# Moving the bias addition of five quads of the first block from ScalarE to VectorE, in a fused cross-attention and FP4 feed-forward kernel

## The reference, cut to what matters

```python
# x: (2, 2048, 512), ctx_1024: (2, 77, 512)
def xattn(features, textual_features, q_masks, Ws, W, w, b, Wcw, bcw, Wcb, bcb):
    txt_proj = einsum('btd,de->bte', textual_features, Ws)
    feat_proj = einsum('bfd,de->bfe', features, W)
    h = tanh(txt_proj[:, None, :, :] + feat_proj[:, :, None, :] + b)      # (2, 2048, 77, 512)
    rho = einsum('bftd,d->bft', h, w[:, 0]) + (1 - q_masks) * NEG
    att = softmax(rho, axis=-1)
    txt_h = einsum('bft,btd->bfd', att, textual_features)
    return tanh(txt_h @ Wcw.T + bcw) * features + tanh(txt_h @ Wcb.T + bcb)

def ffn(x, w_gate, w_up, w_down):            # w_gate, w_up: (1408, 512), w_down: (512, 1408)
    q = fp4_quant_dequant                    # blocks of 16 along the last dim
    h = silu(q(x) @ q(w_gate).T) * (q(x) @ q(w_up).T)
    return q(h) @ q(w_down).T

x = x + xattn(layernorm(x), ctx_1024, ...)
return x + ffn(layernorm(x), w_gate, w_up, w_down)
```

## Time and profile before

| | |
|---|---|
| median of 3 runs | 1590.9 us (1589.16 to 1591.69) |
| the profiled execution | 1591.61 us |
| its span, first to last instruction | 1589.8 us |
| busy: PE / ACT / DVE / POOL | 1452.7 / 1365.2 / 1196.1 / 243.0 us |
| mean granted TensorE clock | 0.976 of 2.4 GHz |
| chain that ended last, by engine | PE 56%, ACT 32%, DVE 9% |

### The profile page before, as it was taken

One profiled execution on the slowest core, in us unless ns is written; L12 is line 12 of the kernel. 1 busy time (PEld: TensorE's weight loads), 2 busy tenths in 40 slices (PEclk: granted clock), 3 DMA queues, 4 the chain that ended last, 5 costly groups with the idle time before them and its releaser, 6 DMA issues.

```text
span 1589.8 us, 24376 instructions
## 1 busy us (share of the span) xinstructions
PE 1452.7 (91%) x9752; PEld 643.9 (41%) x9752; DVE 1196.1 (75%) x1964; ACT 1365.2 (86%) x1258; POOL 243.0 (15%) x406
## 2 busy tenths in 40 slices
PE   6978888866999899997999999899999999889998
PEld 3334444411333333343434444344444444445554
DVE  6599998765586566768676776788878777788887
ACT  5999999999999899998999999989999999233331
POOL 1132222110111011111011111101101111012111
PEclk9989999988999999999999999999999999999999
DMA  4133333230011111202111111111111121123322
GB/s 141 40 80 81 86 80 79 70 75 18 8 26 39 35 30 39 39 14 39 39 39 38 40 39 39 29 36 39 39 39 39 39 39 39 39 52 77 77 66 61
DMA packets 180790, 77.91 MB, mean 49 GB/s; under 512 B 163883, under 2 KB 163883, under 8 KB 180677
## 3 DMA queue, kind: packets, MB, share of 16 engines
q1 hardware_dynamic: 179984, 75.00, 21.0%
q10 hardware_dynamic: 693, 1.36, 0.2%
HBM read 27.85 MB, written 8.39 MB: 23 GB/s over the span
## 4 chain that ended last, share of the span: by engine, by line
PE 56%; ACT 32%; DVE 9%; issue 1%; DMA 1%; POOL 0%; SPq 0%; ACTq 0%; DVEq 0%; POOLq 0%
PE rho L745 20%; ACT hring L570 20%; PE dn L834 9%; ACT hring L565 6%; PE gu0g L822 5%; PE gu1g L822 4%; PE gu0u L822 4%; PE gu1u L822 4%; ACT featT L570 4%; PE gu1u L772 1%; PE gu1g L772 1%; PE gu0u L772 1%; PE gu0g L772 1%; DVE featT L909 1%; ACT featT L565 1%
## 5 line engine op out<-in xcount | busy, mean ns | idle before, releaser
L570 ACT ACTIVATE hring<-featT,bias 128x1024 f32<-128x1024 f32 x880 | 929.6, 1154 | 21.7 <-PE rho L745 21.7
L745 PE MATMUL rho<-hring,wslide 128*32 128x512 f32 x4112 | 507.7, 618 | 86.0 <-ACT hring L570 76.9
L745 PEld LDWEIGHTS rho<-hring,wslide 128*32 128x32 f32 x4112 | 113.4, 111 | 382.5 <-issue 208.6
L834 PE MATMUL dn<-wd_room,turned 128*128 128x512 f16 x1023 | 233.3, 380 | 0.0
L470 POOL TENSOR_SCALAR split_t<-sm 128x88 f32<-128x88 f32 (+2 forms) x91 | 22.4, 246 | 1194.1 <-DVE sm L931 1194.0
L909 DVE TENSOR_SCALAR featT<-featT,bias 128x1024 f32<-128x1024 f32 x264 | 181.0, 749 | 8.2 <-ACT featT L570 3.6
L1210 DVE TENSOR_TENSOR work<-sg,gu1u 128x352 f32<-128x352 f32 x64 | 33.4, 521 | 175.6 <-ACT sg L603 175.2
L834 PEld LDWEIGHTS dn<-wd_room,turned 128*128 128x128 f16 x1023 | 95.2, 98 | 155.5 <-issue 51.1
L822 PE MATMUL gu0g<-wg,turned 128*128 128x352 f16 x768 | 127.6, 317 | 9.6 <-DVE work L1210 8.5
L565 ACT ACTIVATE hring<-featT 128x4096 f32<-128x4096 f32 x35 | 126.6, 3617 | 7.6 <-DVE featT L909 7.6
L822 PE MATMUL gu1g<-wg,turned 128*128 128x352 f16 x768 | 127.0, 316 | 4.8 <-DVE work L1210 4.8
(11 more groups left out here) (192 smaller groups left out, 1523.7 us busy)
## 6 DMA issues: line engine op xcount, KB each, us to landing
xt<-in_x SPq DMA_DIRECT2D x32, 256.0 KB, 2.8
out<-xt SPq DMA_DIRECT2D x32, 256.0 KB, 2.4
work<-in_x SPq DMA_DIRECT2D x10, 512.0 KB, 3.7
xt<-in_x SPq DMA_DIRECT2D x6, 512.0 KB, 3.9
xt<-in_L_ffn_w_gate SPq DMA_DIRECT2D x11, 256.0 KB, 2.6
xt<-in_L_ffn_w_up SPq DMA_DIRECT2D x11, 256.0 KB, 2.7
work<-in_L_ffn_w_down SPq DMA_DIRECT2D x2, 704.0 KB, 4.4
xt<-in_L_ffn_w_down SPq DMA_DIRECT2D x2, 704.0 KB, 4.2
```

The lines of the kernel that those rows point to most:

```text
L570: act.activation(slot[s][:, g, :], featT[:, e, ROW0[k]:ROW0[k] + rows], ACT.Tanh, bias=bias[:, e, base + tok:base + tok + 1]).then_inc(tan ...
L745: last = pe.matmul(rho[SLOTW * g:SLOTW * g + SLOTW, hf * 512:hf * 512 + 512], wslide[:, e, SLOTW - 1 - r:2 * SLOTW - 1 - r], slot[s][:, g, ...
L834: last = pe.matmul(dn[:, :], hqT[:, a, c, :], wd[:, bb, c, :], start=(c == 0 and i == 0), stop=(c == NC - 1 and i == 2))
```

## The change

Five quads of block 0, the numbers 18, 27, 36, 45 and 54 (`HEAD_SUMS`), become summed quads. VectorE makes each sum in a new function `head_sum()`, four TENSOR_SCALARs of 128 x 1024 into `wd_room` (`head_room`), in the rounds w = 1, 3, 5, 7 and 9 between gate_up_weights(w+1, 0) and stats_pair(w+1). ScalarE takes such a quad with one ACTIVATE of 128 x 4096 from there, after it has waited for `summed`. The one room serves all five, so each sum waits until the tanh of the one before is through; and SP's first turning of the down weights into `wd_room` waits for the tanh of quad 54. Blocks 1 to 3 keep the summed quads and the rooms that they had.

```diff
     summed_quads, room_of, room_from = [], {}, {}
+    HEAD_SUMS = [14 + 9 * w // 2 for w in range(1, 10, 2)]
+    for i, m in enumerate(HEAD_SUMS):
+        summed_quads.append(m)
+        room_of[m], room_from[m] = -1, HEAD_SUMS[i - 1] if i > 0 else None
     last_in = {r: QPB * (r + 1) - 1 for r in range(NBLK)}
+    OTHERS = len(HEAD_SUMS)
...
-            room = 0 if k == 1 else 1 + len(summed_quads) % (k - 1)
+            room = 0 if k == 1 else 1 + (len(summed_quads) - OTHERS) % (k - 1)
...
+        head_room = wd_room[:, 0:4096].rearrange("p (g c) -> p g c", g=GRP)
...
             load_wd(1)
+            sp.wait_ge(tanh_ready, GRP * (HEAD_SUMS[-1] + 1))
             for r in range(KC):
                 sp.wait_ge(wdq_ready, r + 1)
...
                 if n in SUMMED:
                     act.wait_ge(summed, GRP * (SUMMED[n] + 1))
                     r = ROW0[room_of[n]]
-                    act.activation(slot[s], featT[:, :, r:r + rows], ACT.Tanh).then_inc(tanh_ready, GRP)
+                    added = featT[:, :, r:r + rows] if room_of[n] >= 0 else head_room
+                    act.activation(slot[s], added, ACT.Tanh).then_inc(tanh_ready, GRP)
                     return
...
+            def head_sum():
+
+                n = summed_quads[sums[0]]
+                if room_from[n] is None:
+                    dve.wait_ge(first_ready, 1)
+                else:
+                    dve.wait_ge(tanh_ready, GRP * (room_from[n] + 1))
+                for g in range(GRP):
+                    r, e = quad_at(n)
+                    dve.tensor_scalar(head_room[:, g, :], featT[:, e, 0:BLOCKS[0]],
+                                      bias[:, e, GRP * r + g:GRP * r + g + 1], None, ALU.add).then_inc(summed, 1)
+                sums[0] += 1
...
             for w in range(NC - 1):
                 copy_pair(w)
                 gate_up_weights(w + 1, 0)
+                if w % 2 == 1:
+                    head_sum()
                 stats_pair(w + 1)
```

## The result

The changed kernel takes 1598.64 us (median of 5 runs, 1597.34 to 1600.07) against 1589.16 for the kernel before in the same series. The medians are 9.5 us apart; the ratio on record is 1.0052, 95% interval 1.0041 to 1.0064, which makes 8.3 us (6.5 to 10.2). The forecast was 6.9 us and 1598; the absolute time is hit more closely than the difference, since the kernel before had 1590.9 us in the series on which the forecast rests. The profiled execution has a span of 1596.8 us, 7.0 longer.

The account below looks back on a forecast made before the run. In the first block VectorE's loop, as long as ScalarE's and TensorE's, would set the pace. Debt of 11.65 us less 3.38 slack less 1.35 regained gives 6.9 us; 1590.9 + 6.9 = 1597.8, said as 1598, range 1594.8 to 1602.5.

Parts of the forecast that it names:

- VectorE's loop as the bound: First block's rounds: VectorE's 19.34 us equal ScalarE's and TensorE's to 0.15 us, so with the sums VectorE sets the pace.
- The debt at turning 10: Five sums of 2.75 us less 2.1 us of waits make stats_pair(10) 11.65 us late; less 3.38 slack, turning 10 8.27.
- ScalarE's gain of 0: Five summed quads save ScalarE at most 3.35 us, which turn into waiting for TensorE, so 0 is taken.
- The 1.35 us regained behind turning 10: From turning 10 to quad 58: 13.95 us instead of 15.3, so quad 58 is late by 6.9 us, not 8.27.
- the rival of the lower clock: Scores behind TensorE's waits run at 1.2 GHz; behind turning 10 this adds 0.6 to 1.6 us; 1600 to 1601, 12%.
- TensorE with 2 us to spare at the even turnings: Five quads need about 20.0 us against VectorE's 22.1, so TensorE waits there 2.1 us for GpSimd.
- turning 10 alone with its 3.4 us of slack decides: At the last turning with a sum, 11.65 us of debt less 3.38 of slack sets the delay carried on.
- The waits that pay for part of the debt: VectorE's former waits for TensorE, 1.0, 0.5 and 0.6 us ahead of rounds 2, 6, 8, take 2.1 us off the debt.
- The rest moves along: Behind quad 58, the softmax and the rest of the kernel move by the same 6.9 us.
- features_pair(9): Behind turning 10: its 5.26 us wait for TensorE absorbs the rest of VectorE's debt, leaving some 0.5 us of wait.
- VectorE's slack covers the sums: Rival: each sum only uses its even turning's 3.38 us and VectorE catches up; ScalarE's saving remains, 1587.6 us, 5%.
- ScalarE waits for the sum: Rival at quad 54: costs nothing until a sum is 3.6 us longer; then a microsecond more, 2%.

Follow-up runs that it names:

- pool_root: Changed kernel with its five sums, but GpSimd makes the three Newton steps of each pair's reciprocal root ahead of its normalising; ratio 1.0075 to the kernel before.
- sums_only: Changed kernel, but ScalarE ignores VectorE's five sums in block 0 and keeps four biased ACTIVATEs a quad; 1599.34 against 1590.19 us before, ratio 1.0056.
- three_sums: Changed kernel with only the first three sums (quads 18, 27, 36; rounds 1, 3, 5); ratio 1.0040 to the kernel before, 6.4 us.
- one_sum: Changed kernel with only the first sum (quad 18, round 1); ratio 1.0017 to the kernel before, 2.7 us.
- act_only: Changed kernel without VectorE's sums in block 0; ScalarE takes the five quads in one ACTIVATE each, biases left out; 1589.42 against 1590.19 us before, ratio 0.9995.

## Why the prediction was right, and where its steps were off

**VectorE's loop as the bound: right in the main.** That a 91% busy engine had no room was read from its waits and its round of 19.34 us. VectorE's half alone costs as much as the whole change, and with another 1.2 us taken from each round the same five sums cost nothing. pool_root shows the limit: there VectorE's round has less work, and the kernel is slower.

**The debt at turning 10: right in size.** Forecast 11.65 us at the end of stats_pair(10), measured 274.06 - 262.82 = 11.2; a sum is 2.65, not 2.75. Turning 10 was to be 8.27 us late and is 8.35 (276.31 - 267.96).

**ScalarE's gain of 0: right within the measurement.** sums_only and the changed kernel differ by less than their intervals; alone it is 0.8 us, at most 2.2. The forecast had ScalarE's waits for TensorE grow by about 10 us in the first block; from 94 to 366 us they grew by 10.8, from 10.2 to 21.0.

**The 1.35 us regained behind turning 10: wrong in size.** It was to be 13.95 us from the turning to quad 58; it took 291.27 - 276.31 = 15.0, mainly since the turning ran at the lower clock (1.9 us instead of 1.1); the rest are a score of 1.92 and 0.15 us up to ScalarE's start, which the sum left out. So 0.35 came back and quad 58 is 8.0 late instead of 6.9. That is the rival of the lower clock, forecast at 0.6 to 1.6 us.

**TensorE with 2 us to spare at the even turnings: wrong.** I had reckoned 20.0 us for five quads at full clock; from turning 5 to turning 6 it took 22.0 (193.16 - 171.16): 1.4 of the 2.0 us more are the score behind the wait, which took 3.31, and 0.3 the projection behind it. So the even turnings didn't wait for GpSimd, only once for 0.5 us, and the waits sum to 12.4 us from turning 2 on, not 15 to 20. The end didn't suffer, since VectorE's round of 22.0 was as long. But the step behind it, that turning 10 alone with its 3.4 us of slack decides, is what three_sums refutes (6.4 us against the 1.5 of that formula). What three_sums showed in its place: each late odd turning pushes TensorE and ScalarE back, and they don't make it up by turning 10. In the changed kernel turning 9 is 7.8 us late already, and turning 10 finds its pair ready 0.5 us before. With five sums both ways of reckoning give nearly the same number, and that this one came out is luck.

**The waits that pay for part of the debt: not sound.** 2.1 us came from an execution with turning 1 at the lower clock; another has 0.2. Against that one, quad 58 of the changed kernel is 10.4 us late (291.27 - 280.91), not 8.0. So the forecast of 6.9 us is low by this term, and the measured 8.3 us is between the two. That one_sum costs 2.7 us fits this, but was not shown apart.

**The rest moves along: right up to the softmax (8.0 us), and nearly to the end.** The profiled pair ends 7.0 apart, the timed runs 8.3 by their ratio. What took 1.7 us back between the two stores shown stays open.

**features_pair(9): too little left.** It was to wait 0.5 us still and waited 2.0, as the debt was 11.2 and the quads 8.0 late.

The rival "VectorE's slack covers the sums" is out, as the slack is a lead and not idle time. "ScalarE waits for the sum" costs nothing in the changed kernel and 8.4 us of waits where the sum stands 4.4 us later.

## What to carry to other kernels

An engine is full when its waits are none, not when its busy share is 100%: with chains of small dependent instructions 91% was full. The slack of a result is a lead that is spent once; a load that repeats in every round eats it and then costs nearly its whole length each time (2.2 to 2.3 of 2.65 us here). And work moved off the busiest engine helps only if the receiver's loop is shorter by more than that work, in most executions and not in the one that was profiled; moving it on to a third engine (pool_root) makes a new wait if that engine stands between the two.

## What the runs showed of the hardware

**VectorE's sum and GpSimd's arithmetic hold each other up.** GpSimd's two TENSOR_SCALARs of 128 x 512 took 1.52 us alone and 3.43 beside VectorE's four of 128 x 1024, and these took 3.11 instead of 2.74: one of its four took 1.10 us, the others about 0.75. The Trainium skill, "SBUF — State Buffer", section "Who interferes with whom", says that a tensor_scalar of VectorE can enter a mode with two ports, which needs the port pair that GpSimd uses, and that the engine that issues later then blocks for the whole instruction. The trace agrees in that both engines have instructions that are longer beside the other's; the mode itself it doesn't show.

**Scores behind a wait are often slow.** With a mean granted clock of 0.96 from 94 to 274 us, single scores of 1.85 us took 3.31, 3.60 and 3.26 us behind the turnings 5, 7 and 9, which had waited 3.55, 3.17 and 3.17 us; the granted clock in these scores was 0.56, 0.52 and 0.57, mostly the lower of the two levels, 1.2 GHz. The first half of the turning between wait and score still took its 0.66 us at full clock. Behind the 1.97 us wait of turning 3 the score took 1.92 us. In sums_only such a stretch fell on the softmax; TensorE's timeline there:

```profile
374.27 2.04 PE L818 MATMUL tr<-gat,stage 128*128 128x128 f32 x8 [1.48 <-DVE stage L1149]
376.25 3.03 PE L753 MATMUL rho<-hring,wslide 128*32 128x512 f32 x16
```

In the profile of act_only the same turning takes 1.13 us, and a score at full clock 1.85. ScalarE waited 2.75 us for the second half of the softmax there instead of 0.28. Where such a stretch falls differs from execution to execution, and it moved the profiled ones by 1.6 us (act_only, quads 62 to 67), 2.4 (the profile before, turning 1) and 2.5 (here), as much as several of the effects sought.

**Many small instructions on GpSimd** follow one another at 0.28 us (the 128 x 2 steps of pool_root), on VectorE at 0.20.
